# Row maxima of attention scores: the mask added by VectorE inside the maximum (batches 1 to 6), and the rows of the first norm written by GpSimd

## The reference

```
x = x + attn(layernorm(x))                      # exp(-|q-k|^2) scores, then a softmax over them
x = x + cross(ctx, ctx, layernorm(x), mask)     # 16 heads of 16, softmax(where(mask==0, min, q k^T) / 4) v
x = x + ffn(layernorm(x))                       # 8 experts, top 2, 256 -> 1024 -> 256
```

## Time and profile before

| | |
|---|---|
| median of 3 runs | 626.04 us (625.72 to 627.48) |
| profiled execution, first to last instruction | 624.3 us |
| TensorE busy | 565.2 us, 91% |
| VectorE busy | 357.6 us, 57% |
| ScalarE busy | 331.2 us, 53% |
| GpSimd busy | 232.7 us, 37% |

### The profile page before, as it was taken

How to read it: one execution, slowest core, us unless ns; L and a number is a source line. 1 busy time by engine, 2 the same in 40 slices (tenths; PEclk the granted TensorE clock), 3 DMA queues, 4 the chain that set the end, 5 groups by cost and what they waited for, 6 DMA issues and landing times.

```text
span 624.3 us, 15593 instructions
## 1 busy us (share of the span) xinstructions
PE 565.2 (91%) x5107; PEld 489.0 (78%) x5108; DVE 357.6 (57%) x841; ACT 331.2 (53%) x726; POOL 232.7 (37%) x301
## 2 busy tenths in 40 slices
PE   4777989999999999977966899999999999999991
PEld 3665767777776777655545899999999999999991
DVE  3637776868788685866756796663323323323331
ACT  4533357565556566523743754456565565565650
POOL 7413121323132221200344635435545545555542
PEclk9969899999999999996996899999999999999997
DMA  8484625261809072552366945766766766757731
GB/s 228 140 111 106 73 58 64 56 101 35 121 22 130 25 108 32 85 101 92 94 200 219 314 147 141 214 170 174 229 191 182 225 181 188 226 174 212 209 92 19
DMA packets 56008, 85.71 MB, mean 137 GB/s; under 512 B 6672, under 2 KB 44720, under 8 KB 55952
## 3 DMA queue, kind: packets, MB, share of 16 engines
q1 hardware_dynamic: 46368, 73.59, 46.5%
q0 software_dynamic: 7872, 10.33, 8.6%
q10 hardware_dynamic: 1712, 1.05, 0.6%
HBM read 62.44 MB, written 9.31 MB: 115 GB/s over the span
## 4 chain that ended last, share of the span: by engine, by line
PE 77%; DVE 7%; ACT 4%; DMA 4%; issue 4%; SPq 2%; POOL 1%; ACTq 0%; POOLq 0%; DVEq 0%
PE pair L2355 22%; PE bank L2395 17%; PE bank L1218 14%; PE pair L1465 5%; PE bank L1604 4%; PE pair L1569 4%; PE pair L1500 2%; PE bank L1187 2%; SPq L1541 2%; DVE row_max L1512 2%; DMA q_stack<-max_lo 2%; PE bank L2319 1%; PE bank L1699 1%; ACT exp_ring L1586 1%; DMA full<-mask_1x1xSxS_ik 1%
## 5 line engine op out<-in xcount | busy, mean ns | idle before, releaser
L2355 PE MATMUL pair<-slots_t,w_now 128*128 128x128 f32 x1248 | 148.1, 278 | 0.0
L2355 PEld LDWEIGHTS pair<-slots_t,w_now 128*128 128x128 f32 x1248 | 144.9, 195 | 0.0
L2365 ACT ACTIVATE hid<-pair,b_tile 128x128 f32<-128x128 f32 x312 | 88.9, 368 | 55.1 <-PE pair L2355 53.6
L2375 DVE TENSOR_TENSOR hid_lo<-hid,hid_hi 128x1024 fp32r<-128x1024 f32 x39 | 47.8, 1225 | 105.4 <-ACT hid_hi L2372 105.4
L2308 POOL DMA_INDIRECT out<-y,scatter_now x39 | 64.0, 1641 | 111.5 <-DMA out<-y,scatter_now 79.0
L1512 DVE TENSOR_REDUCE row_max<-pair 128x4 f32<-128x1024 f32 x64 | 78.0, 1222 | 22.9 <-PE pair L1500 22.9
L2395 PE MATMUL bank<-experts_w,hid_hi 128*128 x624 | 82.6, 285 | 0.0
L1586 ACT ACTIVATE exp_ring<-pair 128x1024 f32<-128x1024 f32 x64 | 65.0, 1028 | 30.4 <-PE pair L1569 27.1
L2395 PEld LDWEIGHTS bank<-experts_w,hid_hi 128*128 128x128 f32 x624 | 75.8, 188 | 0.0
L2293 POOL DMA_INDIRECT slots_in<-xn_rows,gather_now x39 | 42.9, 1099 | 25.9 <-POOL gather_now L2290 15.5
L2372 ACT ACTIVATE hid_hi<-hid 128x512 fp32r<-128x512 f32 x78 | 49.2, 631 | 4.7
(11 more groups left out here) (295 smaller groups left out, 1081.5 us busy)
## 6 DMA issues: line engine op xcount, KB each, us to landing
w_now<-L_ffn_W SPq DMA_DIRECT2D x39, 1024.0 KB, 5.0
experts_w<-L_ffn_W SPq DMA_DIRECT2D x8, 1024.0 KB, 7.8
k_stack<-ck_hi SPq DMA_DIRECT2D x32, 128.0 KB, 4.1
q_stack<-cq_hi SPq DMA_DIRECT2D x32, 128.0 KB, 4.3
ctx_in<-ctx SPq DMA_DIRECT2D x8, 256.0 KB, 2.7
k_stack<-ck_lo SPq DMA_DIRECT2D x16, 128.0 KB, 5.2
q_stack<-cq_lo SPq DMA_DIRECT2D x16, 128.0 KB, 5.2
out<-x SPq DMA_DIRECT2D x7, 256.0 KB, 4.8
```

The source lines that it names most:

```text
L2355: mm = eng.matmul(banks[half][:, f * P:(f + 1) * P], core.w1_now[b.p][:, c, start:start + P], core.slots_t[b.p][:, c, :], start=c == 0, st ...
L2365: act = eng.activation(core.hid[:, g, :], banks[half][:, f * P:(f + 1) * P], ACT.Relu, bias=core.b1_tile[b.p][:, g:g + 1])
L2375: core.m["hid_lo"].at(eng.tensor_tensor(core.hid_lo[b.p][:, :, :], core.hid[:, :, :], core.hid_hi[b.p][:, :, :].bitcast(F32), ALU.subtract))
```

## The change

In batches 1 to 6 the score products start the accumulation themselves and TensorE makes no mask_q products. VectorE replaces its one reduction of a pair by four instructions that each add the bf16 mask to 256 scores (out into the same PSUM place) and take the maximum of the sums into one column of `row_max`. Batches 0 and 7 stay as they were, and so do the mask_k products. From batch 1 on, the rows `xn` of the first norm are written by GpSimd and not by VectorE; VectorE's next moments wait for the norm of the batch before.

```
 def st_moments(core, name, eng, b, it, n):
...
+            core.e["ln0"].wait(eng, b.back(1))
...
 def st_normalise(core, name, eng, b, it, n):
+    if n == 0 and b.v > 0:
+        if name == "vector":
+            return
+        if name == "gpsimd":
+            rstd_done.wait(eng, b)
+            core.e["p_xnT"].wait(eng, b.back(1))
+            for t in range(KT):
+                done.at(eng.tensor_scalar(core.xn[:, t, :], x2_of(core, b)[:, t, :], core.moments[:, 0, t, 0:1],
+                                          core.rstd[:, 0, t:t + 1], ALU.subtract, ALU.mult))
...
+def masked_by_vector(b):
+    return 0 < b.v < NB - 1
...
-    mask_product(core, eng, scores_pair(core, b, i), core.mask_q, core.mask_q_turned)
+    if not masked_by_vector(b):
+        mask_product(core, eng, scores_pair(core, b, i), core.mask_q, core.mask_q_turned)
...
-                            start=False, stop=True, skip_group_check=True)
+                            start=masked_by_vector(b), stop=True, skip_group_check=True)
...
 def st_scores(core, name, eng, b, it, i):
...
+    if masked_by_vector(b):
+        for c in range(KT):
+            for t in range(KT):
+                scores = pair[:, c * 512 + t * S:c * 512 + (t + 1) * S]
+                head = c * PAIRS + i
+                last = eng.tensor_tensor_reduce(out=scores, in0=scores, in1=core.mask_q[:, t, :], scale=1.0,
+                                                scalar=-3.0e38, op0=ALU.add, op1=ALU.max,
+                                                accum_out=core.row_max[:, t, head:head + 1])
+        core.e["maxed"].at(last)
+        return
```

## The result

| | before | after |
|---|---|---|
| median, 20 runs each | 625.99 us (623.72 to 627.58) | 629.04 us (625.99 to 631.26) |
| ratio, 95% interval | | 1.0047 (1.0033 to 1.0061) |
| profiled execution | span 624.3 us | 625.99 us, span 624.3 us |

By the ratio the changed kernel is 2.9 us slower (3.05 between the medians). The profiled execution is the shortest of its twenty, so its profile holds the gains and not the whole loss. Over the runs the mean granted clock of TensorE goes from 0.938 to 0.953, and the longer runs mostly have the lower clocks; in 35 later runs of the kernel before it goes from 0.949 to 0.964.

The account below looks back on a forecast made before the run. TensorE was taken to set the pace, with VectorE's longer maxima then holding it up. Four steady iterations at 6.6 in all, iteration 2 at 1.3 and iteration 7 at 1.9 gave +9.8 us: 635.8 us, range 622.5 to 650.

Parts of the forecast that it names:

- TensorE saves 0.24 per quad: Each quad drops its mask_q products, 0.24 of 1.22 us; eight in an iteration are 1.9 us, 48 in all 11.5.
- M = 1.9: Time of a pair's eight VectorE instructions, start to next instruction's start: 4 x 0.47 us, replacing one reduction's 1.14.
- bounds from below: Lowest estimate of M: 4 x 0.40 = 1.60 us, from plain two-tensor adds at 0.33 plus 0.07 per write-out.
- my three cases: Estimates of M: 1.60 us from below, 1.9 from the nearest row, 2.56 from above with no overlap.
- The walk, 23.8 + 6M: Steady iteration, six maxima on VectorE's path: 1.4 + 9.1 + 0.1 + 13.2 + 6M, if above 31.6; 35.2 at M = 1.9.
- break-even: The M at which the walk's steady iteration equals the old 33.74 us: 1.66.
- Iteration 2, 16.3 + 6M: Length of iteration 2, with less VectorE work: 27.7 us where it was 26.4, so +1.3.
- TensorE's stages fit beside: Iteration 2 after maximum 2: each pair costs only M plus 0.9 us for release, products and start.
- Iteration 7, 11.9 + 8M: Length of iteration 7, which has no next batch: 27.1 us where it was 25.3, given as +1.9.
- The norm: zero: Moving the first norm's rows to GpSimd was counted as no gain and no loss; 4 us was the bound on gain.
- dear end: Highest price assumed for GpSimd's two norm instructions, 1.27 us each; other work covers them up to 1.6 each.
- The granted clock: Sign that the prediction is wrong: TensorE's waits bring its granted clock, 1.00, down; no size given.

Follow-up runs that it names:

- M = 1.82: Mask alone (norm on VectorE) plus one reduction over the bf16 mask behind each pair's four, its result unread; 638.19 us, ratio 1.0177.
- second run: The changed kernel measured again, unchanged, for a second profile; 627.87 us, ratio 1.0031 to the kernel before.

## Why the prediction was right or wrong

It forecast slower, 635.8 us, and it is slower, 629.0, but not for the reason given: with the forecast's mechanism alone the kernel would be faster. That the direction came true is luck. On one chip the mask alone measured 1.0003, the norm alone 1.0024 and both together 1.0031. The intervals are wide, but by these runs the mask's gain is used up by falls of the clock, and the rest of the loss came with the norm, which the forecast had at zero.

- **TensorE saves 0.24 per quad:** right, 0.21 (1.01 us from mask_k to the next stage).
- **M = 1.9:** wrong, 1.48, and outside my bounds from below. The step that failed is "With 0.07 for the write-out, M = 4 x 0.47 = 1.9. I take this, because the new instruction too does two operations on each element". The write-out costs no start of its own, and the main instruction runs 0.38 from start to start, between the plain add's 0.33 and the 0.40 of `cq_lo`. The write-out is a row of its own with 0.14 us, and I had let each of my three cases pay for it. The Trainium skill (VectorE: DVE Perf Modes, the section on the TRN2 errata) gave an estimate of 1.8, also too long; its section on the DRAIN, taken at its word, does not hold for these rows, where a main instruction starts together with a write-out of 0.14 us. The rows agree with the Trainium skill's section on two Vector instructions with no wait between them (same page), which lets an instruction start before the one ahead has finished if it is not held; I had not applied it to the write-out.
- **The walk, 23.8 + 6M:** right where VectorE sets the pace: 34.7 for 34.8 at M = 1.82. At M = 1.48 it gives 32.7 for 33.2, since behind maximum 5 it is no longer VectorE that TensorE waits for: in iteration 5 the last write-out of that maximum starts at 201.39, and TensorE, which never stands still there, comes to the products of quad 6 only at 201.91. The break-even lies between 1.59 (the straight line through the two measured points, 33.23 and 34.80) and 1.65 (down from 34.80 with the walk's 6 us per us), an estimate, not at 1.66. At M = 1.82 the forecast's sum is 632.7, and 638.2 was measured, with falls in three iterations: even with the right M the time would have been missed by them.
- **Iteration 2, 16.3 + 6M:** 25.2 at M = 1.48, and 26.64 was measured without a fall. From maximum 0 to 2 it holds (7.55 for 7.56). Behind that "TensorE's stages fit beside" was wrong: maximum 4 comes 3.2 us after maximum 3 instead of 2.4, behind ScalarE's part of cq. **Iteration 7, 11.9 + 8M:** 23.7, measured 24.77 without a fall.
- **The norm: zero.** Right for iterations 3 to 7, where GpSimd's row is 1.23, near the dear end that I had tested. In iteration 0 there is no cover, and the products behind it start 1.5 us later than before. I had tested the cover in one steady iteration only. The term was put at zero, and norm alone measured 1.5 us (1.0024); only the delay in iteration 0 is seen in the rows, and that it makes up the 1.5 is not shown.
- **The granted clock:** I named a fall as what would make the prediction wrong and gave it no price. It is the largest item. Without falls the sum is -2.0 for iterations 3 to 6, +0.2 and -0.5 for 2 and 7, and between nothing and 1.5 for the norm: -2.3 to -0.8 us. One fall adds 2.2 or 3.5, both 5.7; the measured +2.9 lies within what this gives, but no profile of the changed kernel shows both. I had priced waits of TensorE by their length, which in iterations 2 and 7, where I counted them only inside M, leaves out what comes behind.

Shown is that every fall in the table's last column stands behind such waits, and that the kernels that move masks and shorten or avoid the waits have no fall in their profiles, one each, and are faster. That the waits cause the falls is argued from this and not shown for a single execution. In iteration 2 three of the four profiles with all pairs of batch 1 on VectorE show a fall, in iteration 7 four of the six with all of batch 6; of the eight with neither, none. What decides between two executions with the same waits is open.

## What to carry to other kernels

Before pricing an instruction that also writes a reduced column, look for a row of such a pair or assume that the write-out hides behind the next instruction; the length of a row is not its price, the distance of starts is. Move work to a less busy engine piece by piece: six of eight pairs gave 0.9% where all eight gave nothing, and the two left behind were the ones that TensorE waited for (no run left two others behind). And price a new wait of TensorE by iteration, the thin ones first, with the clock that may follow it: waits of 1.5 to 1.8 us in sum where there had been 0.7 led to 2.2 to 3.5 us more in some executions.

## What was unexpected in the hardware

- The write-out of the accumulated maximum (0.14 us) starts together with the next main instruction of VectorE and adds nothing to the distance of starts, 0.38 us; a 128x256 add with maximum, one operand in PSUM and one bf16, takes 0.38 us from start to start, the first of four 0.34.
- With waits alike within 0.03 us, one execution keeps 2.4 GHz and another falls to 1.2 GHz: for some 6.8 us in iteration 2 of the changed kernel (9.5 us at a mean of 0.64), and for the last 8.8 us of iteration 7 in its second run. No single wait in the 5 us ahead of these falls is over 1.07 us, and the 1.13 us at the start of iteration 2 (and 1.13 in the changed kernel) is followed by full clock for 9 us.
- GpSimd's `xn` row of 128x256 with two column operands takes 1.23 us, as long as its 128x512 add (1.28).
